# Splitting the context loads of a Perceiver cross-attention over two DMA queues

## The reference

```python
def _L0_xattn_ref(query, key):
    a = jnp.einsum('bqd,bkd->bqk', query, key)
    e = jax.nn.softmax(a, axis=-1)
    c = jnp.einsum('bqk,bkd->bqd', e, key)
    return c
...
x = x + _L0_xattn_ref(_layernorm(x, axis=-1), ctx_4096)
x = x + _L0_attn_ref(_layernorm(x, axis=-1), L0_attn_w_q, L0_attn_w_k, L0_attn_w_v, L0_attn_w_o)
x = x + _L0_ffn_ref(_layernorm(x, axis=-1), L0_ffn_A_w, L0_ffn_B_w, L0_ffn_Wq_w, L0_ffn_keys)
```

## Time and profile before

| | |
|---|---|
| median of three runs | 1615.15 us |
| profiled execution | 1612.68 us |
| its span | 1610.9 us |
| cross-attention within the span | about 0 to 520 us |
| TensorE, VectorE, ScalarE, GpSimd busy | 92%, 48%, 31%, 39% |
| context loads: DMAs on SyncE's queue | 464, and 8 for left-over keys |

### The profile page before, as it was taken

The page is one execution under the profiler, slowest core; times in us unless marked ns, Lnnn a source line. Parts: engine busy times, 40 slices in busy tenths (PEclk is TensorE's granted clock), DMA queues, the critical chain, the costliest instruction groups (busy, mean ns, idle before and its releaser), DMA issues.

```text
span 1610.9 us, 24088 instructions
## 1 busy us (share of the span) xinstructions
PE 1478.6 (92%) x9593; PEld 1044.2 (65%) x9593; DVE 777.1 (48%) x1095; ACT 505.8 (31%) x698; POOL 625.3 (39%) x282
## 2 busy tenths in 40 slices
PE   1698988888889699999999999999999999999999
PEld 0233333333333388888888888888888888878777
DVE  2456646647655320446544644644465440357323
ACT  1032433433433422332423423323323332222221
POOL 0031422413405324366466564663663663430000
PEclk9899999999899799999999999999999999999999
DMA  9999899989985423233133233323331343230023
GB/s 233 247 216 227 203 255 255 216 252 254 226 238 123 139 102 108 79 105 105 56 106 98 78 104 104 102 85 99 104 104 55 106 152 105 79 105 1 29 76 131
DMA packets 182222, 219.96 MB, mean 137 GB/s; under 512 B 9488, under 2 KB 107792, under 8 KB 179504
## 3 DMA queue, kind: packets, MB, share of 16 engines
q1 hardware_dynamic: 182144, 218.87, 50.1%
HBM read 207.82 MB, written 10.49 MB: 136 GB/s over the span
## 4 chain that ended last, share of the span: by engine, by line
PE 76%; DMA 8%; DVE 6%; SPq 5%; issue 2%; ACT 2%; DVEq 0%; POOL 0%; ACTq 0%
PE ps L729 15%; PE ps L731 14%; PE ps L730 14%; PE ps L666 11%; DMA xa_raw<-in_ctx 8%; SPq L305 5%; PE ps L1769 5%; PE ps L1771 5%; PE ps L1770 5%; DVE xa_kt L520 2%; PE ps L642 2%; PE ps L1709 2%; PE ps L1862 1%; DVE xa_kt L524 1%; PE ps L1734 1%
## 5 line engine op out<-in xcount | busy, mean ns | idle before, releaser
L729 PE MATMUL ps<-h_hi,w_hi 128*128 128x512 f32 x800 | 315.4, 394 | 1.2 <-DVE h_lo L1425 1.1
L731 PE MATMUL ps<-h_hi,w_lo 128*128 128x512 f32 x800 | 311.7, 390 | 0.0
L730 PE MATMUL ps<-h_lo,w_hi 128*128 128x512 f32 x800 | 311.5, 389 | 0.0
L1157 POOL TENSOR_TENSOR w_lo<-raw,w_hi 128x2048 fp32r<-128x2048 f32 (+1 forms) x52 | 212.7, 4095 | 254.4 <-ACT w_hi L1222 213.8
L474 POOL TENSOR_TENSOR xa_x<-xa_x,xa_tmp 64x512 f32<-64x512 f32 x120 | 150.3, 1269 | 360.0 <-ACT xa_tmp L403 348.1
L622 PE MATMUL ps<-xa_kt,xa_q_t 128*64 128x416 f32 (+2 forms) x1024 | 211.1, 557 | 78.7 <-DVE xa_kt L520 56.4
L520 DVE STREAM_TRANSPOSE xa_kt<-xa_raw 128x832 f32<-128x832 f32 (+1 forms) x208 | 193.9, 995 | 158.4 <-PE ps L622 102.9
L622 PEld LDWEIGHTS ps<-xa_kt,xa_q_t 128*64 128x64 f32 x1024 | 71.8, 146 | 208.1 <-issue 134.5
L666 PE MATMUL ps<-xa_raw,xa_e_t 32*64 32x512 f32 (+1 forms) x3264 | 184.1, 593 | 0.0
L729 PEld LDWEIGHTS ps<-h_hi,w_hi 128*128 128x128 f32 x800 | 150.2, 188 | 36.4 <-issue 6.4
L1513 DVE TENSOR_TENSOR rows<-rows,ps 128x512 f32<-128x512 f32 x168 | 115.5, 688 | 116.3 <-PE ps L1771 116.3
(11 more groups left out here) (222 smaller groups left out, 1894.3 us busy)
## 6 DMA issues: line engine op xcount, KB each, us to landing
xa_raw<-in_ctx SPq DMA_DIRECT2D x128, 320.0 KB, 8.5
xa_raw<-in_ctx SPq DMA_DIRECT2D x144, 256.0 KB, 11.0
raw<-in_L_attn_w_q SPq DMA_DIRECT2D x32, 1024.0 KB, 5.9
raw<-in_L_attn_w_o SPq DMA_DIRECT2D x30, 1024.0 KB, 5.0
xa_raw<-in_ctx SPq DMA_DIRECT2D x64, 192.0 KB
xa_raw<-in_ctx SPq DMA_DIRECT2D x64, 128.0 KB
raw<-in_L_attn_w_k SPq DMA_DIRECT2D x8, 1024.0 KB, 5.2
raw<-in_L_attn_w_v SPq DMA_DIRECT2D x8, 1024.0 KB, 5.2
```

The lines of the kernel that those rows point to most:

```text
L729: pe.matmul(out, hi, mov_hi, start=first, stop=False)
L730: pe.matmul(out, hi, mov_lo, start=False, stop=False)
L731: return pe.matmul(out, lo, mov_hi, start=False, stop=last)
L1157: pool.tensor_tensor(w_lo[:, n % 2, part], raw[:, n % 2, part], w_hi[:, n % 2, part].bitcast(F32), ALU.subtract).then_inc(w_lo_done, 1)
```

## The change

Quadrants 0 and 1 of every unit are still issued by SyncE, quadrants 2 and 3 now by ScalarE, on its own DMA queue. SyncE keeps its order of units and pieces; within a piece it issues quadrant 0 and then 1. ScalarE issues the loads of all five places ahead of its first instruction. In the stages it waits for a piece of both sides before it goes to the next piece: `refill(s, g)` takes piece g of unit 2s + 5 and then piece g of unit 2s + 6. In even stages the three refills stand at the head of `evacuate`; in odd stages the first stands after the fourth of the eight moves in `first_half_moved`, the others at the head of `evacuate`.

```diff
-QUAD_ORDER = (0, 2, 1, 3)
+QUEUE_QUADS = ((0, 1), (2, 3))
...
+    def load_unit_piece(eng, queue, u, g):
...
+        for i in QUEUE_QUADS[queue]:
+            for j0, j1 in piece_runs(x, g, i):
+                k0 = KEY0[x] + a * COLS[x] + SQ * j0
+                src = ctx[b, k0:k0 + SQ * (j1 - j0), i * 512:(i + 1) * 512].rearrange("(k c) n -> c k n", c=SQ)
+                eng.dma_start(raw[quadrant(i), at + j0:at + j1, :], src).then_inc(raw_in[place(u)][g], 16)
+        if queue == 0 and g == NPIECE - 1 and has_left(u):
...
-                load_unit_piece(u, g)
+                load_unit_piece(sp, 0, u, g)
...
+        def refill(s, g):
+
+            for a in range(SIDES):
+                u = SIDES * s + a + PLACES
+                if u < UNITS:
+                    products(act, s, g, [a])
+                    load_unit_piece(act, 1, u, g)
+
         def first_half_moved(b):
             act.wait_ge(ga_ready, b + 1)
             for k in range(A_OPS):
+                if k == A_OPS // 2:
+                    refill(HALVES * b + 1, 0)
                 slot_free(tmp_no(b, k))
...
         def evacuate(s):
             b, x = divmod(s, HALVES)
+            for g in range(x, NPIECE):
+                refill(s, g)
             products(act, s)
...
+        for u in range(PLACES):
+            for g in range(NPIECE):
+                load_unit_piece(act, 1, u, g)
         normalize_rows(0)
```

More of the change, by code:

```diff
@@ L294, in part_of @@
         return own(b) if k % 2 == 0 else other(b)
-    def cross_sync(sp, aside):
[L297 to L310, removed]
+    def load_unit_piece(eng, queue, u, g):
+        s, a = divmod(u, SIDES)
+        b, x = divmod(s, HALVES)
+        at = UNIT * place(u)
+        for i in QUEUE_QUADS[queue]:
[4 more added lines that the diff above has]
+        if queue == 0 and g == NPIECE - 1 and has_left(u):
+            if u == 2:
+                eng.wait_ge(left_clear, 1)
+            left = ctx[b, LEFT_KEY, :].rearrange("(i n) -> i n", i=QUADRANTS)
+            eng.dma_start(raw[0:P:SQ, at + LEFT_BLOCK, :], left).then_inc(raw_in[place(u)][g], 16)
+    def cross_sync(sp, aside):
         def load_rows(t):
```

## The result

The changed kernel is slower: 1665.8 us (median of 4 runs) against 1615.5 (median of 4), a ratio of 1.0302 with a 95% interval of 1.0272 to 1.0332. Its profiled execution has a span of 1666.0 us, 55.1 more than before.

What follows compares the result with a forecast made beforehand. It took each cross-attention stage as a loop whose late link is the landing of the context refill. Loops +51.8 us and start -11 gave +41 on the profiled 1612.7, forecast as 1653 us; 8 in 10 range 1590 to 1735.

Steps and rivals of the forecast that it cites:

- The rate: Context loads on two queues: between 240 and 400 GB/s, taken as 340, so 170 for whoever gets half.
- Rival A: Context loads on two queues stay near 240 to 280 GB/s; 1698 to 1760 us, chance 0.20.
- The order: ScalarE's refills: last urgent bytes stand behind two pieces not needed yet; +2.8 us in even stages, +3.1 in odd.
- The lateness: ScalarE's first refill: +1.9 us behind four moves in odd stages, +3.2 behind the normalization in stages 2, 6, 10.
- signs of being right: Among the signs expected in the profile after: odd loops and stages 2, 6, 10 worse than stage 0.
- Stages 4, 8, 12 and 5, 9: Loops: the former +2.8 less 1.6 for the x1 store on SyncE's queue, +3.6 in all; odd ones +5.0 each.
- Stage 13: Loop with one unit only to refill: nothing urgent waits behind anything, its wait goes, -2.6 us.
- The start: Prefill until stage 1's data are complete: 53 us at 340 GB/s, -11 us; ScalarE's late first normalization costs nothing.
- Issues on ScalarE at no cost: Odd stages: 11 issues take 4.7 us against 6.7 of cover, counted as nothing; without cover up to 2 us each.

Runs made afterwards that it cites:

- e8: The changed kernel with the quadrants dealt out otherwise: SyncE takes 0 then 2, ScalarE 3 then 1; 1729.9 us.
- e4: The changed kernel with the queues' quadrants exchanged: SyncE takes 0 and 2, ScalarE 1 and 3; 1719.8 us.
- e1: The changed kernel with ScalarE's refills reordered: all pieces of urgent unit 2s+5 first, then those of 2s+6; 1599.6 us.
- e7: The kernel before, all on SyncE's queue, with refills in the changed kernel's ScalarE order, piece by piece of both units; 1733.9 us.
- e2: The changed kernel with ScalarE's first refill ahead of the eight moves in odd stages and ahead of the normalization in stages 2, 6, 10; 1680.3 us.
- e3: The changed kernel with ScalarE normalizing the first rows and moving the queries after two units' loads, before issuing the other three; 1653.1 us.

## Why the prediction was right, and where not

The direction, the size and the mechanism held: 1653 forecast, 1665.8 measured. Its terms held less well than their sum. Growth of the loops against before, us:

| stages | forecast | measured |
|---|---|---|
| 0 | +2.8 | +2.7 |
| 1, 3, 7, 11 | +20.0 | +17.6 |
| 2, 6, 10 | +18.0 | +6.7 |
| 4, 8, 12 | +3.6 | +10.7 |
| 5, 9 | +10.0 | +18.9 |
| 13 | -2.6 | -0.2 |
| all | +51.8 | +56.5 |

That the sum comes so near is in part luck: 11 us too many in stages 2, 6 and 10 stand against 16 too few in 4, 5, 8, 9 and 12.

- *The rate*, 340 between 240 and 400: 341 in the prefill, 297 to 340 in the loops. The upper end, 400, was not reached. The port halves that the Trainium skill has in "SBUF — State Buffer", "Door 1: The DMA port swizzle", agree with two queues that keep to different halves giving 340 for 240.
- *Rival A* falls with these rates. The Trainium skill's sentence behind it ("DMA: Bandwidth & Descriptors", "Issuing engines are not separate DMA queues") fits e8 (233) and the loops of e4, but neither e4's prefill (302, where one queue had 237) nor the change.
- *The order*, +2.8 and +3.1 us a stage, the higher rate already taken off: stage 0 +2.7; e1 takes 63 us out of the loops, e7 shows 122 on one queue.
- *The lateness* was one of two steps that failed. It was put at 3.2 us in stages 2, 6 and 10, as if ScalarE issued when the normalization ends. Stage 2 after the change (timeline):

```profile
140.44 12.23 SPq L305 DMA_DIRECT2D xa_raw<-in_ctx  x14
141.96 2.09 ACT L356 ACTIVATE xa_xn<-xa_x,xa_rs 128x2048 f32<-128x2048 f32 x1 [5.53 <-DVE xa_rs L508]
142.09 9.61 ACTq L305 DMA_DIRECT2D xa_raw<-in_ctx  x15
```

The refill behind the normalization goes out 0.13 us after that starts, while it runs until 144.05. That is 6.5 us after the values' start (135.59), where SyncE before issued after 5.2: 1.3 late. These stages came out no worse than stage 0, though that they would be was among the signs of being right; e2, which takes their lateness away, gains 0.8 to 1.9 us in each. In odd stages the 1.9 for the first piece gave about the right sum, but what counts there is when the last urgent pieces are issued (e2).

- *Stages 4, 8, 12 and 5, 9*, the other step, carry 1 MB more on SyncE's queue: a store in the former, a load of x in the latter. The prediction took 1.6 us off for the store, as it stays on SyncE's queue, and counted nothing for the load. But these transfers run beside ScalarE's last urgent piece. The queues while that piece is under way (packets, MB, share), SyncE's (q1) in stage 0 (81.29 to 93.92) and 8 (359.77 to 376.09), then SyncE's and ScalarE's (q10) in stage 1 (116.31 to 128.30) and 5 (254.13 to 270.06):

```profile
q1 hardware_dynamic: 1251, 2.28, 52.7%
q1 hardware_dynamic: 1527, 3.30, 56.9%
```

```profile
q1 hardware_dynamic: 1169, 2.11, 56.9%
q10 hardware_dynamic: 1046, 1.83, 47.8%
q1 hardware_dynamic: 1211, 2.98, 63.6%
q10 hardware_dynamic: 1073, 1.90, 40.5%
```

SyncE's queue moves 0.9 to 1.0 MB more and the last piece takes longer, 16.3 us for 12.6 in stage 8 and 15.9 for 12.0 in stage 5, though in stage 5 it goes out as soon after the values' start as in stage 1 (14.5 and 14.4 us). On one queue that load of x was issued behind the urgent unit. No run without these rows was made.

- *Stage 13* was to lose its 2.6 us wait and has 3.2.
- *The start* was mis-sized: -11 forecast, -3.9 measured. ScalarE was to be through its 38 issues at 25 us, with 4.3 MB of its 8.3 moved; it was at 40.06, and by then its queue had moved 5.67 (0 to 40.06):

```profile
q10 hardware_dynamic: 3164, 5.67, 43.3%
```

So 2.6 MB were still queued, where 4.0 were counted, and the queue moved slower: 142 GB/s from the start on and not 170. The queries then came after the data, and the overlap that was to cost nothing cost the gain. In e3 the first values start 16.8 us earlier than before, 6 more than forecast.

- *Issues on ScalarE at no cost* held for the changed kernel, whose loops wait for context, and stopped holding in stages 1 and 3 once the landing was repaired (e1).

The loops came to +56.5 for +51.8, the start to -3.9 for -11, and the rest of the span, for which nothing was forecast, to +2.5: together +55 for +41.

## What to carry to other kernels

A second queue can raise the rate and still lengthen the loop: count the bytes that stand in each queue ahead of the last one that somebody waits for, and divide by that queue's share. What other queues carry at that moment counts too: with 1 MB more on SyncE's queue, ScalarE's last piece took up to 4 us longer. Split by quadrant so that each queue keeps to its half of the partitions, and let both serve the urgent tile first. A compute engine that issues loads issues them in its own program order: put what it must compute early ahead of a long prefill.

## What was not expected of the hardware

Two queues over the same quadrants, merely dealt out otherwise, ran at 233 and 302 GB/s in the prefill against 341. And ScalarE's issue is no fixed 0.45 us: in the prefill, with earlier loads of its queue still under way, single ones took up to 3.15 us, and the 38 took 39 us, in which it did nothing else (durations min/median/max in ns):

```profile
L305 ACTq DMA_DIRECT2D xa_raw<-in_ctx x240: 317/450/3151, 0.8 to 539.9; - x120
```
